# State space layer: one 256x256 product formed at the start in place of two projections in every batch

## What is computed

```python
xz = jnp.einsum('bld,ed->ble', x, in_proj_w)
x_in, z = jnp.split(xz, 2, axis=-1)
xc = conv(swapaxes(x_in)) + conv_b            # 4 taps along the tokens
x_in = _silu(jnp.swapaxes(xc, 1, 2))
dbc = jnp.einsum('bld,ed->ble', x_in, x_proj_w)
delta_in = dbc[..., :D_INNER]                 # 256 wide
Bp = dbc[..., D_INNER:D_INNER + D_STATE]      # 16 wide
Cp = dbc[..., D_INNER + D_STATE:]             # 16 wide
delta = jax.nn.softplus(jnp.einsum('bld,ed->ble', delta_in, dt_proj_w) + dt_proj_b)
...
h = exp(dt * A) * h + dt * bt * xt            # step by step over the tokens
y = jnp.einsum('bds,bs->bd', h, ct) + D * xt
```

## Time and profile before

| | us |
|---|---|
| Median of 3 runs | 3571.08 |
| The three runs | 3568.99, 3571.08, 4755.25 |
| The profiled execution | 3569.22 |
| Its span in the profile | 3568.0 |
| PE busy, DVE busy, ACT busy, POOL busy | 2400.9, 2647.3, 1584.8, 1204.8 |

### The profile page before, as it was taken

The page is one execution under the profiler, slowest core; times in us unless marked ns, Lnnn a source line. Parts: engine busy times, 40 slices in busy tenths (PEclk is TensorE's granted clock), DMA queues, the critical chain, the costliest instruction groups (busy, mean ns, idle before and its releaser), DMA issues.

```text
span 3568.0 us, 35108 instructions
## 1 busy us (share of the span) xinstructions
PE 2400.9 (67%) x8963; PEld 1196.9 (34%) x8963; DVE 2647.3 (74%) x7051; ACT 1584.8 (44%) x3364; POOL 1204.8 (34%) x1118
## 2 busy tenths in 40 slices
PE   2338287847767578856878577665887578775854
PEld 1005123523224332524335332334324243344313
DVE  4874796878878787888878788887878788773182
ACT  1415353644435543744536543545427444442332
POOL 2110042522416134442435134251434315341461
PEclk7558588968979689967889679787889689887957
DMA  3000111122112211222121311122112221203112
GB/s 87 1 5 13 33 30 53 36 61 73 48 40 56 59 55 42 56 45 89 39 58 40 76 52 45 44 54 70 47 37 61 49 82 45 53 22 94 53 48 83
DMA packets 118909, 181.38 MB, mean 51 GB/s; under 512 B 15824, under 2 KB 55392, under 8 KB 115552
## 3 DMA queue, kind: packets, MB, share of 16 engines
q1 hardware_dynamic: 114528, 170.05, 17.6%
q0 software_dynamic: 4096, 8.40, 0.8%
HBM read 156.51 MB, written 21.89 MB: 50 GB/s over the span
## 4 chain that ended last, share of the span: by engine, by line
DVE 33%; PE 23%; issue 18%; POOL 9%; ACT 8%; DMA 6%; SPq 2%; DVEq 1%; POOLq 0%; ACTq 0%
DVE wmask L677 9%; DMA qk<-bounce 3%; DVE best L813 3%; POOL gat L1521 3%; PE ps_rest L1195 2%; PE ps_att L619 2%; PE ps_rest L1205 2%; ACT wmask L657 2%; PE ps_att L928 2%; DVE wmask L804 2%; POOL slots L1637 2%; ACT z L639 1%; POOL cols L1769 1%; PE ps_rest L1664 1%; DVEq L815 1%
## 5 line engine op out<-in xcount | busy, mean ns | idle before, releaser
L677 DVE TENSOR_SCALAR_CACHE_REDUCE wmask<-z,tc 128x512 bf16<-128x512 f16 x880 | 606.5, 742 | 69.1 <-ACT z L639 60.0
L845 POOL TENSOR_SCALAR wmask<-wmask 128x512 bf16<-128x512 bf16 x256 | 161.2, 630 | 935.7 <-DVE wmask L804 927.9
L1265 POOL TENSOR_TENSOR gat<-sil,cbs 128x512 f32<-128x512 f32 x256 | 323.7, 1269 | 249.4 <-ACT sil L1230 128.4
L619 PE MATMUL ps_att<-qk 128*128 128x512 bf16 x512 | 248.2, 489 | 230.0 <-ACT z L639 90.8
L657 ACT ACTIVATE wmask<-z,tc 128x512 bf16<-128x512 f16 x400 | 283.6, 711 | 104.5 <-DVE tc L719 96.5
L639 ACT ACTIVATE z<-ps_att,row_scale 128x512 f16<-128x512 f32 x256 | 175.8, 687 | 336.1 <-PE ps_att L619 292.2
L1205 PE MATMUL ps_rest<-rest_hT,WF 128*128 128x512 f32 x512 | 290.2, 653 | 46.8 <-ACT sil L1230 42.7
L1230 ACT ACTIVATE sil<-ps_rest,w_b1T 128x512 f32<-128x512 f32 x256 | 173.4, 684 | 305.3 <-PE ps_rest L1205 297.6
L1195 PE MATMUL ps_rest<-gat,WP 128*128 128x512 f32 x512 | 285.5, 643 | 9.7 <-POOL gat L1265 9.3
L928 PE MATMUL ps_att<-z,Vp 128*32 128x128 f32 x2048 | 275.9, 280 | 13.7 <-DVE both_parts L1000 13.7
L1534 POOL TENSOR_TENSOR rest_c<-rest_c,hg 128x512 f32<-128x512 f32 x128 | 162.4, 1269 | 331.5 <-DVE hg L1493 329.5
(11 more groups left out here) (331 smaller groups left out, 5083.1 us busy)
## 6 DMA issues: line engine op xcount, KB each, us to landing
cbs<-spreads SPq DMA_DIRECT2D x128, 256.0 KB, 3.3
WF<-in_w SPq DMA_DIRECT2D x64, 256.0 KB, 2.6
WP<-in_w SPq DMA_DIRECT2D x64, 256.0 KB, 2.6
WF<-in_wfc SPq DMA_DIRECT2D x64, 256.0 KB, 2.7
WG<-in_wgate SPq DMA_DIRECT2D x64, 256.0 KB, 3.0
WP<-in_wproj SPq DMA_DIRECT2D x64, 256.0 KB, 3.2
qk<-bounce SPq DMA_DIRECT2D x32, 384.0 KB, 5.6
bounce<-both_parts SPq DMA_DIRECT2D x72, 128.0 KB
```

The costliest lines, as they stand in the source:

```text
L619: return pe.matmul(bank[:], qs[:, h, j * P:(j + 1) * P], ks[:, h, :], start=True, stop=stop)
L677: od.up(dve.tensor_scalar(wmask[:, i, :], z16[:, i % HT, :], tc[:, 0, i:i + 1], None, ALU.is_ge, ALU.add, accum_out=tc[:, 1, i:i + 1]))
L1265: weighed0.up(pool.tensor_tensor(gat[m % 2], sil[m % 2], cbs[e % 2][:], ALU.mult))
```

## The change

At the start, when the weights have arrived, PE turns the four 128x128 blocks of the first projection, DVE copies them to `rest.c[0]`, PE multiplies them with `dt_projT` into `rest.bank[2]`, and DVE writes the 256x256 product over the first projection in `x_projT`. Each batch then multiplies `xi` once by that product, and its result is `dt_ps` at once. Of every batch, four matmuls (L1299), the two ACT copies (L1334) and their waits are gone. The 96 columns of B and C stay as they were.

```diff
--- before.py
+++ after.py
@@ -138,6 +138,7 @@
     gbo = sb("gbo", [P, B]); bo2 = sb("bo2", [P, 1])
     gbh = sb("gbh", [P, B]); gbb = sb("gbb", [P, B, E])
     wiped, turnedP, gbs = sig("wiped", 5, 16), sig("turnedP"), sig("gbs", 2)
+    turnedX, keptX, joinedX, onestep = sig("turnedX"), sig("keptX"), sig("joinedX"), sig("onestep")
     Aneg = sb("Aneg", [P, DC, NS])
 
 
@@ -254,7 +255,7 @@
     hid = [flat(hfc2)[:, wide + u * CAP:wide + (u + 1) * CAP] for u in range(2)]
     xpad = [sb(f"xpad{k}", [P, 3 + S]) for k in range(DC)]
     xi, sz, dl, dtx = (cols[:, n] for n in range(4))
-    din, yz = hfc, hg
+    yz = hg
     rowsB = rest.hT[0:NS]
     spreadsB = nc.dram_tensor("spreads", (NS, S), F32, kind="Internal").ap()
     dA, dBx, hs, hc = (rest.bank[0], rest.bank[3]), gat + [rest.c[0][:], rest.c[1][:]], hfc, hg
@@ -265,7 +266,7 @@
     spread0, cb0, up0, gated, weighed0, down0 = sig("spread0", E), sig("cb0", E), sig("up0", E * FC), sig("gated", E * FC), sig("weighed0", E * FC), sig("down0", E * FC)
     y0, out0 = sig("y0"), sig("out0", 2)
     proj_in, split_in, conved, xed = sig("proj_in", 4), sig("split_in", 4), sig("conved", 2), sig("xed", 2)
-    din_ps, dins, dt_ps, dts = sig("din_ps", 2), sig("dins", 2), sig("dt_ps", 2), sig("dts")
+    dt_ps = sig("dt_ps", 2)
     soft, softe, logged, stepped, y_open, zeroed = sig("soft"), sig("softe"), sig("logged"), sig("stepped"), sig("y_open"), sig("zeroed")
     keptB, outB, spreadB, spreadC = sig("keptB"), sig("outB", 1, 16), [sig(f"spreadB{i}", NS // 4, 16) for i in range(4)], sig("spreadC", NS)
     decays, inputs, scans, seen, summedY = sig("decays", 2 * NS), sig("inputs", 2 * NS), sig("scans", 2 * NS), sig("seen", 2 * NS), sig("summedY", NS)
@@ -375,7 +376,21 @@
         ready.up(dve.tensor_scalar(gbo[:], modT[0][:, :, 2], bo2[:], None, ALU.mult))
 
     def pe_late():
+
         turnedP.up(pe.transpose(rest.bank[0][:, 0:E], wts["bproj"][:], ident[0:E, 0:E]))
+        for k in range(DC):
+            for m in range(DC):
+                mm = pe.transpose(in_tiles(rest.bank[1])[:, DC * k + m, :], wts["x_projT"][:, k, m * P:(m + 1) * P], ident[:])
+        turnedX.up(mm)
+        yield 1.5
+        yield keptX.at(0)
+        pe.wait_ge(*keptX.at(0))
+        for k in range(DC):
+            for m in range(DC):
+                mm = pe.matmul(rest.bank[2][:, k * DI:(k + 1) * DI], in_tiles(rest.c[0])[:, DC * k + m, :], wts["dt_projT"][:, m, :],
+                               start=m == 0, stop=m == DC - 1)
+        joinedX.up(mm)
+        yield 2.2
 
     def dve_late():
 
@@ -383,6 +398,15 @@
         dve.wait_ge(*turnedP.at(0))
         gbs.up(dve.tensor_tensor(gbb[:], modT[1][:, :, 5:6].broadcast_to([P, B, E]),
                                  rest.bank[0][:, 0:E].rearrange("p (a e) -> p a e", a=1).broadcast_to([P, B, E]), ALU.mult))
+        yield 0.4
+        yield turnedX.at(0)
+        dve.wait_ge(*turnedX.at(0))
+        keptX.up(dve.tensor_copy(rest.c[0][:], rest.bank[1][:]))
+        yield 0.7
+        yield joinedX.at(0)
+        dve.wait_ge(*joinedX.at(0))
+        onestep.up(dve.tensor_copy(wts["x_projT"][:, :, 0:DI], rest.bank[2][:].rearrange("p (k m) -> p k m", k=DC)))
+        yield 1.0
 
     def started(eng):
 
@@ -1284,21 +1308,17 @@
             if m == 0:
                 yield split_in.all(b)
                 pe.wait_ge(*split_in.all(b))
+                if b == 0:
+                    yield onestep.at(0)
+                    pe.wait_ge(*onestep.at(0))
             for k in range(DC):
                 mm = pe.matmul(bk[m][:], wts["x_projT"][:, k, m * P:(m + 1) * P], xi[:, k, :], start=k == 0, stop=k == DC - 1)
-            din_ps.up(mm)
+            dt_ps.up(mm)
             yield 2.18
         for k in range(DC):
             mm = pe.matmul(bk[2][0:96, :], wts["x_projT"][:, k, DI:DI + 96], xi[:, k, :], start=k == 0, stop=k == DC - 1)
         stack_ps.up(mm)
         yield 2.18
-        yield dins.all(b)
-        pe.wait_ge(*dins.all(b))
-        for m in range(DC):
-            for k in range(DC):
-                mm = pe.matmul(bk[m][:], wts["dt_projT"][:, k, m * P:(m + 1) * P], din[k], start=k == 0, stop=k == DC - 1)
-            dt_ps.up(mm)
-            yield 2.18
         yield stacks.at(b, 1)
         pe.wait_ge(*stacks.at(b, 1))
         pe.matmul(bk[2][:], zero_bf[:, 0:P], zero_bf[:], start=True, stop=False)
@@ -1328,11 +1348,6 @@
                 act.wait_ge(*out1.all(b - 1))
             xed.up(act.activation(xi[:, k, :], c[k][1][:], ACT.Silu, bias=wts["m_cb"][:, k:k + 1]))
             yield 0.77
-        for m in range(DC):
-            yield din_ps.at(b, m)
-            act.wait_ge(*din_ps.at(b, m))
-            dins.up(act.activation(din[m], bk[m][:], ACT.Copy))
-            yield 0.64
         yield stack_ps.at(b, 1)
         act.wait_ge(*stack_ps.at(b, 1))
         keptB.up(act.activation(rowsB, bk[2][0:NS, :], ACT.Copy))
@@ -1884,8 +1899,7 @@
         pe.wait_ge(*late.all(0))
         yield hot.all(0)
         pe.wait_ge(*hot.all(0))
-        pe_late()
-        yield 0.2
+        yield from pe_late()
         for b in every:
             yield from pe_mixture0(b)
             yield from pe_experts0(b)
@@ -1909,8 +1923,7 @@
         yield late.all(0)
         dve.wait_ge(*late.all(0))
         yield turnedP.at(0)
-        dve_late()
-        yield 0.4
+        yield from dve_late()
         for b in every:
             yield from dve_mixture0(b)
             yield from dve_experts0(b)
```

## The result

The changed kernel takes 3581.88 us in the median of 20 runs, the kernel before 3574.05 us in as many beside them: ratio 1.0023, 95% interval 1.0013 to 1.0032. It is slower by 8 us, where 12 us less were forecast. The spans of the profiled executions are 3578.6 and 3568.0 us.

The account below looks back on a forecast made before the run. No engine is full; two chains, attention and the previous batch's rest, share engines in fixed order. From 3569.22 us, 0 - 3.5 - 9 gave 3557, 3559 on the runs' median, stated as 3560; range 3532 to 3592.

Parts of the forecast that it names:

- Direct gain 0: In each batch's front, the removed PE matmuls and ACT copies win 0 us, bounds 0 and 38 us.
- Rival 3: Over all batches, the removed instructions count in full, 38 us, giving 3533 us; chance 0.08.
- Start 0: At the kernel's start, the added transposes, matmuls and copies cost 0, or 6 us if their cover were gone.
- Tail, -9 us: After the attention's end, the rest alone is 12 us shorter; net gain 9 us, bounds 0 and 12.
- the 3 us that its pairs cost elsewhere: The six pairs moved from after the attention to beside it cost 0.5 us each there, 3 us.
- Scans out of the softmax, -10.5 us: In batches 3 to 6, 21 scans move ahead of the softmax and give back 10.5 us.
- the prediction's price of 0.5 us for a scan with its product: Beside the softmax tiles, each scan with its product costs 0.5 us.
- It applies in full to batch 6 and in part to 4 and 5; two batches' worth is 0 to 14 us, and I take the middle, 7 us: Front among the attention's last choices: its added PE matmuls L1288 and L1292 delay the attention by 7 us.
- Rival 4: In batches 4 to 6, the front blocks the choices through DVE's waits: 34 us lost, 3605 us; chance 0.15.
- the prediction's 0 for the softmax: PE's clock at the softmax: removing L1299 from the hole before it costs 0, as it starts slow already.

Follow-up runs that it names:

- Run 1: The changed kernel's work with every engine's instruction list in the order of the kernel before; ratio 1.0001 to the kernel before.
- run 9: The kernel before, in its own order, with the four matmuls L1299 carried out twice in every batch; ratio 1.0016 to the kernel before.
- run 2: The kernel before's work (L1299 and its two copies back) with the lists in the changed kernel's order; ratio 1.0055 to the kernel before.
- run 12: The changed kernel with share 534 and, for batches 3 and 5, the front's matmuls not placed before the eleventh softmax tile; ratio 1.0116 to the kernel before.

## Why the prediction was wrong

- **Direct gain 0: right.** Run 1 shows it within 4 us, and run 9 the cover. One reading was loose: L1299 began 0.8 us before the split and not wholly beside it; its first 0.8 us lie beside the ACT copy L1338, for which DVE waited. Rival 3 (3533 us) was wrong as a whole, but right that among the choices L1299 counts nearly in full, 3.1 to 3.8 us in each of three batches. Its reason was not: the earlier trace rows is of a stretch that lies for the most part before the last eight choices, and in these PE is busy for 60% in the changed kernel and for 64% in run 2 (25.86 of 40.70 us in attention 7), which has L1299 there.
- **Start 0: right.** The first softmax tile is as early as before.
- **Tail, -9 us: right in sign and size.** The rest alone became 12.5 us shorter, 12 forecast before the 3 us that its pairs cost elsewhere.
- **Scans out of the softmax, -10.5 us: a second step that failed.** The 21 scans do stand ahead of the softmax of attentions 4 to 7, but they are not missing beside it: later scans move up into their place. Between the first and the last softmax tile of these four attentions DVE has 85 scans and 78 products before (and in run 1), and 82 and 81 in the changed kernel. By the prediction's price of 0.5 us for a scan with its product that is worth 1.5 us at the most. Measured against run 1, the four softmax phases change by +1.7, -2.9, -2.7 and -2.1 us, 6.0 us shorter in all. That this lies near the forecast is luck; why they are shorter is open.
- **"It applies in full to batch 6 and in part to 4 and 5; two batches' worth is 0 to 14 us, and I take the middle, 7 us": the step that failed.** It was 24.3 us in the last eight choices of three attentions, and 30.9 us over their choices in all; outside its bounds. I had priced only L1288 and L1292 on PE. Left out were L1279 (now L1303, 6.06 us in one row above), the convolution and split on DVE, which was busy for 20.83 of 30.00 us in those choices already, and that such a block falls between the steps of one tile and delays the whole chain from DVE over POOL to PE. And I counted batches 4 and 5 as parts, though batch 4's convolution and L1303 stood among the choices, and in batch 5 the whole front up to the bias step did. How the 24.3 us divide between these was not measured.
- **Not seen at all:** the search of attention 7, the time before its first choice, became 8.5 us longer than in run 1; those of 4 to 6 became 10.3 us shorter. Up to 2780 us the changed order was 4 us ahead of run 1 in the attention; it lost 18.8 us in the last one. The trace shows where in that search; these are two of its matmuls L643 on PE, one after the other in the changed kernel:

```profile
2836.35 0.63 PE L643 MATMUL ps_att<-qk 128*128 128x512 bf16 x1
...
2847.80 0.38 PE L643 MATMUL ps_att<-qk 128*128 128x512 bf16 x1
```

L643 came every 1.2 to 2.5 us up to there. In the 11.5 us between these two, PE worked on the experts' L1679, L1681 and L1693. The last of the search's seventeen L643 started 70.6 us after the end of attention 6, in run 1 (there L647) 58.3 us. So this too is the order, at a place that has nothing to do with the front; that it makes the whole 8.5 us was not tested.
- **Rival 4 was the nearest**, with the right place and 34 us as its price. Its "full" form, DVE waiting for `keptB` among the choices, was not what happened: those waits fell to 19.0 us. It happened in run 12.

The measured terms against run 1, which has the same work: +30.9 for the choices and -7.7 for the softmax of attentions 5 to 7, -12.9 for the tail, so +10.3 us; the other phases return 8.6 us, 7.0 of them in attentions 0 to 3, and the two profiled spans differ by 1.7 us. The ratios, over many runs, differ by 0.22%, or 8 us: the profiled execution of the changed kernel lies 2.0 us below its median and that of run 1 1.2 us above. So the place and the rough size of each term are measured, in one execution each, and their sum only to within some 6 us.

## What to carry to other kernels

When a hand-set order is steered by assumed costs and shares, taking work out also changes the order, for every batch a little more; correct the share in the same edit, or measure the removed work in the old order first. A block moved to another phase is to be priced by all that it issues on each engine and by the chain that it cuts, not by the busy time of one engine. Here the cheapest place for a block with waits of its own was a stretch in which the other chain waited for a DMA, as long as only one block stood in it.

## What was not expected of the hardware

PE work of 29 us in all (L1299, eight batches) cost nothing within 4 us where a split on DVE lay over it. A second copy of it at the same place cost some 6 us, and among the choices of three batches it cost 10.3 us, at 3.4 us for each 3.60, though PE was busy for only 64% there (run 2, attention 7): in that stretch the idle time of PE did not make added PE work free. Its removal also left PE's clock in the softmax much as it was, though L1299 stood in the hole ahead of it. The first 10 us of the last softmax of the kernel before, by windows (the clock is the first number behind POOL's):

```profile
3089.46:3099.46 10.00, 8.63 (x38) 4.96 (x37) 8.28 (x16) 7.51 (x20) 3.64 (x4) 0.66 0.18 47
```

And of run 1, in the same order without L1299:

```profile
3097.71:3107.71 10.00, 8.63 (x36) 4.89 (x35) 8.03 (x16) 7.37 (x19) 4.64 (x5) 0.63 0.15 52
```

The granted clock is 0.66 and 0.63, in both cases a mean between its two levels, 0.50 (1.2 GHz) and 1.00 (2.4 GHz); two softmax phases earlier it is 0.57 before and 0.66 in run 1, the other way round. In the changed kernel it is 0.64 at this place. So whether L1299 stood in the hole or not shows no effect of one sign on the clock behind it, and nothing here speaks against the prediction's 0 for the softmax. The choices it did not look at: there the mean granted clock of the last eight fell from 0.89 to 0.73 when the front came among them.
